# Attention weights read straight from PSUM: the copy to SBUF on ScalarE is dropped in a fused attention and FFN kernel

## The chip, the cores and the metric

One Trainium2 chip, 8 cores. Each core runs the same program on its own 4096 of the 32768 tokens; nothing is exchanged between cores. The metric is the device time of the slowest core in microseconds (us). Engines: PE is TensorE, DVE is VectorE, ACT is ScalarE, POOL is GpSimd, SP is SyncE. "Granted clock" is TensorE's clock as a share of 2.4 GHz.

## The reference

```python
q = x @ Wq + bq;  kv = (x @ Wdown + bdown) @ Wup + bup        # 16 heads of 64
att = softmax(einsum('bthd,btgd->bthg', rope(q), rope(k)) / 8)  # heads against heads, per token
out = einsum('bthg,btgd->bthd', att, v) @ Wout + bout
x = layernorm(x + out)
h = silu(x @ wg.T) * (x @ wu.T)                                 # 1024 -> 3072
x = layernorm(x + h @ wd.T)
```

Attention is between the 16 heads of one token, so there is no token by token score matrix: each token has 16 x 16 weights. The rotation of q and k by one token's own position leaves their product as it is, so the kernel leaves it out.

## The kernel before

Activations lie transposed, features on the 128 partitions and tokens along the free dimension. After a stage that casts the weights to bf16 (until about 340 us), a core works through 8 tiles of 512 tokens. `XC` is 8, the number of 128-feature blocks; `HF` is 256, half a tile.

Per tile s there are two streams of work. The main chain: `plan_head` (x load, latent and q projections), then for each half `hf` K and V (`plan_kv_part`), the scores (`plan_sc`), the weighted sum (`plan_av`) and the output projection (`plan_wo`), then the first layer norm. The second stream, `plan_ffn_ch2`, is the FFN of tile s-1: gate (L388, PSUM bank P0) and up (L398, P1) projections, `h = silu(gate) * up` (ScalarE L407, VectorE L414), down projection (L441, P2), second layer norm. The first layer norm of tile s waits for the second of tile s-1. Tile 0's attention has no FFN beside it, and the last FFN no attention.

`plan_av` works as follows. For a head the exponentials `e_sb` lie on 16 partitions (one per query head). For each block J of 128 features (two query heads) and each pair gp of key heads, one matmul with the selection matrix `selz_sb` (L707) spreads 16x512 weights over the 128 partitions into bank P5 or P6, alternating. ScalarE copies them as bf16 to `erep[gp % 2]` (L680). VectorE multiplies with the values `vdup` into `p_sb[gp % 2]` (L663). Two matmuls with the identity `id_sb` (L723) add the halves of `p_sb` into bank P7; after 8 pairs VectorE copies P7 to `avn` (L667). So a half has 8 x 8 = 64 such steps, and the kernel 1024. The order on PE within a block is b0 b1 b2 g0 g1 b3 g2 g3 b4 g4 g5 ... b7 g10 g11 g12 ... g15, where b is a broadcast and two g belong to one step.

P5 and P6 serve the projections, K, V, scores and output projection too, each of which waits for the last reader of the bank.

The order in which each engine issues is computed when the program is built. Every operation is added with `add(stream, fn, waits, inc, d=...)`, where d is its assumed cost in ns (default PE 260, VectorE 510, ScalarE 700; the summing matmuls 152, the ScalarE copy 810). The main chain and the FFN each keep their own order on each engine; a list scheduler merges the two. It takes next the operation that can start earliest by these costs, in classes of 100 ns, and among equal ones that with the longest remaining path:

```python
key = (round(es / 100.0), -CP[id(nd)], es)
if best is None or key < best[0]:
    best = (key, k, ch, nd, es)
```

At run time each engine executes its list in order, waiting on semaphores.

Of the kernel before, what the change touches and what calls it, by code (L numbers as in the profile page):

```python
# [11 lines left out]
AF = mybir.ActivationFunctionType  # L12
# [13 lines left out]
XC = D // 128  # L26
# [16 lines left out]
def build_nc(nst=NST):  # L43
# [30 lines left out]
    with ctx:  # L74
# [56 lines left out]
        s_pe = Sem(ctx, nc, "s_pe")  # L131
# [141 lines left out]
        def plan_head(s):  # L273
            t0 = s * ST
            xcast_c = []
            for c in range(XC):
                w = []
                if c == 0:
                    if ck['kv_pe_end']:
                        w.append((s_pe, ck['kv_pe_end']))  # L280
                    if ck['wo_stt_end']:
                        w.append((s_v, ck['wo_stt_end']))
                dst = x_bf[:, c * ST:(c + 1) * ST]
                src = xt[c * 128:(c + 1) * 128, t0:t0 + ST]
                w = [(s_x[c % 2], s_x[c % 2].c)] + w
                add('G', (lambda e, d=dst, sr=src: e.dma_start(d, sr)),
                    waits=w, inc=s_x[c % 2], n=16)
                xcast_c.append((s_x[c % 2], s_x[c % 2].c))
            xc_store[s] = xcast_c

            pe0 = s_pe.c
            for m in range(2):
                for c in range(XC):
                    w = []
                    if m == 0:
                        w.append(xcast_c[c])
                        if c == 0:
                            if ck['erep_end']:
                                w.append((s_s, ck['erep_end']))
                            if ck['avn_h1']:  # L300
                                w.append((s_v, ck['avn_h1']))
                    o = P[5 + m][:, :]
                    l = wd_sb[:, m * 1024 + c * 128:m * 1024 + (c + 1) * 128]
                    r = x_bf[:, c * ST:(c + 1) * ST]
                    add('T', (lambda e, o=o, l=l, r=r, st=(c == 0), sp=(c == XC - 1):
                              e.matmul(o, l, r, start=st, stop=sp)),  # L306
                        waits=w, inc=(s_pe if c == XC - 1 else None))
            lat_evac = []
            for m in range(2):
                w = [(s_pe, pe0 + m + 1)]  # L310
                if m == 0 and ck['kv_pe_end']:
                    w.append((s_pe, ck['kv_pe_end']))
                o, i_ = lat_bf[:, m * ST:(m + 1) * ST], P[5 + m][:, :]
                b = bdn_sb[:, m:m + 1]
                lat_evac.append(add('S', (lambda e, o=o, i=i_, b=b:
                                          e.activation(o, i, AF.Identity, bias=b)),
                                    waits=w, inc=s_s))
            lat_done = s_s.c

            ld0 = [s_ld[0].c, s_ld[1].c]  # L320
            pe0, sc0 = s_pe.c, s_s.c
            for m in range(XC):
                w = []
                if m < 2:
                    if ck['wqb_rd']:
                        w.append((s_pe, ck['wqb_rd']))
                else:
                    w.append((s_pe, pe0 + m - 1))
                dst, src = wqb[m % 2][:, :], wq_s[:, m * 1024:(m + 1) * 1024]
                dma('Y', s_ld[m % 2], dst, src, w)  # L330
            for m in range(XC):
                w = [(s_ld[m % 2], ld0[m % 2] + 16 * (m // 2 + 1))]
                w.append((s_s, lat_done if m < 2 else sc0 + m - 1))
                for c in range(XC):
                    o = P[5 + m % 2][:, :]
                    l = wqb[m % 2][:, c * 128:(c + 1) * 128]
                    r = x_bf[:, c * ST:(c + 1) * ST]
                    add('T', (lambda e, o=o, l=l, r=r, st=(c == 0), sp=(c == XC - 1):
                              e.matmul(o, l, r, start=st, stop=sp)),  # L339
                        waits=(w if c == 0 else ()), inc=(s_pe if c == XC - 1 else None))  # L340
            ck['wqb_rd'] = s_pe.c
            q_evac_v = []
            for m in range(XC):
                w = [(s_pe, pe0 + m + 1)]
                if m == 0 and ck['had_end']:
                    w.append((s_v, ck['had_end']))
                o, i_ = q_sb[:, m * ST:(m + 1) * ST], P[5 + m % 2][:, :]
                b = bq_sb[:, m:m + 1]
                q_evac_v.append(add('S', (lambda e, o=o, i=i_, b=b:
                                          e.activation(o, i, AF.Identity, bias=b)),  # L350
                                   waits=w, inc=s_s))
            ck['q_evac_last'] = q_evac_v[-1]
            return q_evac_v[-1]
# [161 lines left out]
        for s in range(nst):  # L515
# [30 lines left out]
            prev_wout_v = [0] * XC  # L546
            prev_avn_end_hf0 = 0

            def plan_kv_part(hf, part):
                pe0, sc0 = s_pe.c, s_s.c  # L550
                wgt = wupk_sb if part == 0 else wupv_sb
                for g in range(NH):
                    w = []
                    if g < 2:
                        w += list(wT([]))
                    if sc0 + g - 1 > 0:
                        w.append((s_s, sc0 + g - 1))
                    for c in range(2):
                        o = P[5 + g % 2][:, 0:HF]
                        l = wgt[:, g * 256 + c * 128:g * 256 + (c + 1) * 128]  # L560
                        r = lat_bf[:, c * ST + hf * HF:c * ST + hf * HF + HF]
                        add('T', (lambda e, o=o, l=l, r=r, st=(c == 0), sp=(c == 1):
                                  e.matmul(o, l, r, start=st, stop=sp)),  # L563
                            waits=(w if c == 0 else ()), inc=(s_pe if c == 1 else None), d=152)
# [62 lines left out]
            def plan_av(hf, exp_end, kv_evac_g, guard=()):  # L627
# [7 lines left out]
                v_norm = v0 + 4  # L635
                v_tt = lambda J, gp: v0 + 4 + J * 9 + gp + 1
                v_avn = lambda J: v0 + 4 + (J + 1) * 9
                s_evac = lambda lin: sc0 + lin + 1

                eap = e_sb[0:16, 0:NH * HF].rearrange("p (g t) -> p t g", g=NH)  # L640
                add('V', (lambda e, o=esum32[:, :], i=eap:
# [10 lines left out]
                prev_esum_v = s_v.c  # L652
                for J in range(XC):
                    for gp in range(8):
                        w = [(s_s, s_evac(J * 8 + gp))]
                        if gp >= 2:
                            w.append((s_pe, pe_gsum(J, 2 * gp - 3)))
                        elif J >= 1:
                            w.append((s_pe, pe_gsum(J - 1, 13 + 2 * gp)))
                        o = p_sb[gp % 2][:, :]  # L660
                        a = erep[gp % 2][:, :]
                        b = vdup[hf][:, gp * 512:(gp + 1) * 512]
                        add('V', (lambda e, o=o, a=a, b=b: e.tensor_mul(o, a, b)),  # L663
                            waits=w, inc=s_v)
                    o = avn[:, J * HF:(J + 1) * HF]
                    i_ = P[7][:, 0:HF]
                    add('V', (lambda e, o=o, i=i_: e.tensor_copy(o, i)),  # L667
                        waits=[(s_pe, pe_gsum(J, NH - 1)), (s_v, s_v.c)], inc=s_v)
                ck['avtt_end'][hf] = v_tt(XC - 1, 7)
                prev_avn_end = s_v.c  # L670
                for J in range(XC):
                    for gp in range(8):
                        lin = J * 8 + gp
                        w = list(wS([(s_pe, pe_bcast(J, gp))]))
                        if lin >= 2:
                            J2, gp2 = divmod(lin - 2, 8)
                            w.append((s_v, v_tt(J2, gp2)))
                        o = erep[gp % 2][:, :]
                        i_ = P[5 + gp % 2][:, :]
                        add('S', (lambda e, o=o, i=i_: e.activation(o, i, AF.Identity)),  # L680
                            waits=tuple(w), inc=s_s, d=810)
                erep_end = s_s.c
                for J in range(XC):
                    sched = [('b', 0), ('b', 1), ('b', 2), ('g', 0), ('g', 1)]
                    for gp in range(3, 8):
# [3 lines left out]
                    for kind, idx2 in sched:  # L689
# [8 lines left out]
                        if kind == 'b':  # L698
                            gp = idx2
                            lin = J * 8 + gp  # L700
                            if lin >= 2:
                                w.append((s_s, s_evac(lin - 2)))
                            o = P[5 + gp % 2][:, :]
                            l = selz_sb[:, J * 128:(J + 1) * 128]
                            r = e_sb[:, gp * 512:(gp + 1) * 512]
# [18 lines left out]
                                waits=w, inc=s_pe, d=152)  # L724
                assert s_pe.c == pe0 + XC * 24
                assert s_v.c == v0 + 4 + XC * 9
                assert s_s.c == sc0 + XC * 8
                prev_av_pe_end = s_pe.c
                if hf == 0:
                    prev_avn_end_hf0 = prev_avn_end  # L730
# [49 lines left out]
            vd0 = plan_kv_part(0, 1)  # L780
            exp_end0, had0 = plan_sc(0, kd0)
            avn_end0, erep_end0 = plan_av(0, exp_end0, vd0)
            kd1 = plan_kv_part(1, 0)
            vd1 = plan_kv_part(1, 1)
            exp_end1, had1 = plan_sc(1, kd1)
            wo0 = plan_wo(0, avn_end0, [(s_s, exp_end1)])
            avn_end1, erep_end1 = plan_av(1, exp_end1, vd1, [(s_v, wo0[-1])])
            wo1 = plan_wo(1, avn_end1, [(s_s, erep_end1)])
            ck['kv_pe_end'] = s_pe.c
            ck['had_end'] = had1  # L790
            ck['avn_h1'] = avn_end1
# [258 lines left out]
```

How the kernel before makes its waits and increments, by code:

```python
            @blk.sync  # L144
            def _(sync):
                srcs = [(bq_sb[:, :], bq_d[:, :]), (bdn_sb[:, :], bdn_d[:, :]),
                        (bupk_sb[:, :], bupk_d[:, :]), (bupv_sb[:, :], bupv_d[:, :]),
                        (bout_sb[:, :], bout_d[:, :]), (cvec_sb[:, :], cvec_d[:, :]),
                        (stg[0][:, 0:128], selred_d[:, :]),
                        (stg[0][:, 128:256], ones_d[:, :]),
                        (stg[0][:, 256:384], id_d[:, :]),
                        (stg[1][0:16, 0:1024], selz_d[:, :])]
                for j, (dst, src) in enumerate(srcs):
                    s_ld[j % 2].inc(sync.dma_start(dst, src), 16)
                sync.wait_ge(s_ld[0].h, s_ld[0].c)
                sync.wait_ge(s_ld[1].h, s_ld[1].c)
# [38 lines left out]
            @blk.sync  # L195
            def _(sync):
                for j, (src, soff, dt, kind, dst, doff) in enumerate(pieces):
                    if j >= 2:
                        sync.wait_ge(s_v.h, v0 + j - 1)
                    dstap = stg[j % 2][:, :]
                    if dt == I32:
                        dstap = dstap.bitcast(I32)
                    s_ld[j % 2].inc(sync.dma_start(dstap, src[:, soff:soff + 1024]), 16)
# [1 line left out]
            @blk.vector  # L205
            def _(vector):
                for j, (src, soff, dt, kind, dst, doff) in enumerate(pieces):
                    vector.wait_ge(s_ld[j % 2].h, ld0[j % 2] + 16 * (j // 2 + 1))
                    srcap = stg[j % 2][:, :]
                    if dt == I32:
```

## Time and profile before

| | us |
|---|---|
| median of the runs | 3688.32 (3687.78 to 3688.86) |
| the profiled execution | 3682.43 |
| its span on the slowest core | 3680.8 |
| spans of the 8 cores | 3661.5 to 3680.8 |
| mean granted clock of the cores | 0.898 to 0.903 |

The profile is of one execution on the slowest core. In its views a row of several equal instructions ("x2") gives the start of the first and their united busy time; rows of matmuls overlap, so the distance of starts is the better measure of PE. A line number is that of the kernel's source. An idle time is put down to what ended it.

### The profile page before, as it was taken

To read this page: it belongs to the slowest core of one execution; us is meant where nothing else is said; L and a number is where in the kernel's file an instruction comes from. 1 tells how busy PE (TensorE), PEld (TensorE's weight loads), DVE (VectorE), ACT (ScalarE), POOL (GpSimd) and SP (SyncE) were. 2 spreads that over 40 slices of the span, in tenths; PEclk is the share of its full clock that TensorE was granted. 3 is DMA by queue.
4 is the path that set the end of the run, shared out by engine and by line. 5 is a ranking of instruction groups with operands and counts; after the bars stand their busy time and mean duration, and the time that the engine had idled before them with its cause. 6 is when DMAs were issued, how large, how long until landed. Compare 5 with 4: busy or idle time off the path is not lost.

```text
span 3680.8 us, 44636 instructions; the slowest of 8 cores (3661.5 to 3680.8 us)
## 1 busy us (share of the span) xinstructions
PE 2729.1 (74%) x12447; PEld 1088.1 (30%) x12672; DVE 1465.2 (40%) x2246; ACT 1366.8 (37%) x2353; POOL 292.3 (8%) x540
## 2 busy tenths in 40 slices
PE   0001787788877988698968896898779897889666
PEld 0000222233333333233323332333333333333222
DVE  2221434354444434444335343544444444544302
ACT  0000353355334624363445442563346343534201
POOL 0111000001000110001000100011000100110010
PEclk9999756789988999999988998899989998899778
DMA  7886000212241133212231224113321332122322
GB/s 199 242 240 180 21 1 24 60 39 64 84 102 43 52 89 91 71 48 83 79 93 41 83 75 106 35 52 97 88 62 48 89 89 69 52 83 73 95 77 86
DMA packets 108728, 304.16 MB, mean 83 GB/s; under 512 B 16192, under 2 KB 24768, under 8 KB 108496
## 3 DMA queue, kind: packets, MB, share of 16 engines
q1 hardware_dynamic: 61520, 169.14, 16.3%
q0 software_dynamic: 46976, 132.15, 12.7%
q8 instruction: 118, 1.93, 0.2%
q14 instruction: 114, 0.93, 0.1%
HBM read 269.77 MB, written 39.85 MB: 84 GB/s over the span
## 4 chain that ended last, share of the span: by engine, by line
PE 56%; DMA 13%; issue 8%; ACT 7%; DVE 6%; another core or an unknown queue 0%; SPq 0%; DVEq 0%; ACTq 0%; POOL 0%; POOLq 0%
PE P L441 9%; PE P L707 8%; PE P L398 8%; PE P L388 8%; PE P L723 7%; PE P L622 7%; PE P L563 4%; DMA x_bf<-xt 3%; DMA wgb<-wg_s 3%; DMA wub<-wu_s 3%; DMA wqb<-wq_s 2%; ACT erep L680 2%; PE P L339 2%; PE P L762 2%; DVE esum L642 2%
## 5 line engine op out<-in xcount | busy, mean ns | idle before, releaser
L680 ACT ACTIVATE erep<-P 128x512 bf16<-128x512 f32 x1024 | 602.5, 597 | 635.4 <-PE P L707 458.8
L663 DVE TENSOR_TENSOR p_sb<-erep,vdup 128x512 bf16<-128x512 bf16 x1024 | 432.9, 425 | 563.8 <-PE P L723 272.1
L388 PE MATMUL P<-x_bf,wgb 128*128 128x512 bf16 x1458 | 494.0, 422 | 136.3 <-DMA wub<-wu_s 115.3
L398 PE MATMUL P<-x_bf,wub 128*128 128x512 bf16 x1466 | 512.1, 410 | 36.0 <-DVE h_sb L414 33.2
L723 PE MATMUL P<-p_sb,id_sb 128*128 128x256 bf16 x2048 | 464.9, 296 | 22.7 <-DVE p_sb L663 15.4
L707 PE MATMUL P<-e_sb,selz_sb 16*128 16x512 bf16 x1024 | 418.4, 422 | 67.2 <-DVE e_sb L650 46.4
L441 PE MATMUL P<-h_sb,wdb 128*128 128x512 bf16 x1482 | 443.0, 381 | 14.0 <-DVE r_bf L450 10.5
L597 DVE TENSOR_TENSOR hadb<-q_sb,krep 128x2048 bf16<-128x2048 bf16 x256 | 310.4, 1224 | 350.1 <-ACT krep L578 181.5
L306 PE MATMUL P<-x_bf,wd_sb 128*128 128x512 bf16 x127 | 59.0, 564 | 418.2 <-DMA x_bf<-xt 416.7
L622 PE MATMUL P<-hadb,selred_sb 128*16 128x256 bf16 x2048 | 322.9, 279 | 47.4 <-ACT e_sb L609 20.2
L414 DVE TENSOR_TENSOR h_sb<-s_sil,P 128x512 bf16<-128x512 bf16 x192 | 131.4, 684 | 460.8 <-PE P L398 253.2
L407 ACT ACTIVATE s_sil<-P 128x512 bf16<-128x512 f32 x192 | 114.4, 596 | 449.0 <-PE P L388 448.4
L762 PE MATMUL P<-avn,wob 128*128 128x256 bf16 x1024 | 237.9, 286 | 36.7 <-DMA wob<-wout_s 23.0
L388 PEld LDWEIGHTS P<-x_bf,wgb 128*128 128x128 bf16 x1536 | 147.7, 104 | 364.2 <-issue 293.5
L723 PEld LDWEIGHTS P<-p_sb,id_sb 128*128 128x128 bf16 x2048 | 179.1, 100 | 244.5 <-issue 164.7
L398 PEld LDWEIGHTS P<-x_bf,wub 128*128 128x128 bf16 x1536 | 151.3, 102 | 257.7 <-issue 183.8
L256 POOL DMA_DIRECT2D wgb<-wg_s x192 | 105.1, 547 | 1498.2 <-PE P L398 1385.8
L622 PEld LDWEIGHTS P<-hadb,selred_sb 128*16 128x16 bf16 x2048 | 157.2, 90 | 201.8 <-issue 174.5
L707 PEld LDWEIGHTS P<-e_sb,selz_sb 16*128 16x128 bf16 x1024 | 88.3, 92 | 366.7 <-issue 366.6
L339 PE MATMUL P<-x_bf,wqb 128*128 128x512 bf16 x504 | 134.2, 416 | 81.9 <-DMA wqb<-wq_s 68.3
L609 ACT ACTIVATE e_sb<-P,cvec_sb 16x256 bf16<-16x256 f32 x256 | 116.4, 464 | 197.4 <-PE P L622 196.8
L441 PEld LDWEIGHTS P<-h_sb,wdb 128*128 128x128 bf16 x1536 | 127.8, 97 | 177.6 <-issue 87.6
(65 smaller groups left out, 1913.2 us busy)
## 6 DMA issues: line engine op xcount, KB each, us to landing
wdb<-wdn_s SPq DMA_DIRECT2D x64, 768.0 KB, 4.3
wgb<-wg_s POOLq DMA_DIRECT2D x192, 256.0 KB, 3.0
wub<-wu_s POOLq DMA_DIRECT2D x192, 256.0 KB, 3.0
wob<-wout_s SPq DMA_DIRECT2D x128, 256.0 KB, 2.9
wqb<-wq_s SPq DMA_DIRECT2D x64, 256.0 KB, 3.1
yt<-x2b SPq DMA_DIRECT2D x64, 256.0 KB, 3.4
stg<-wg SPq DMA_DIRECT2D x24, 512.0 KB, 5.3
stg<-wu SPq DMA_DIRECT2D x24, 512.0 KB, 5.2
```

The lines of the kernel that those rows point to most:

```text
L339: e.matmul(o, l, r, start=st, stop=sp)),
L388: e.matmul(o, l, r, start=st, stop=sp)),
L398: e.matmul(o, l, r, start=st, stop=sp)),
L441: e.matmul(o, l, r, start=st, stop=sp)),
L563: e.matmul(o, l, r, start=st, stop=sp)),
L597: add('V', (lambda e, o=o, a=q3, b=b: e.tensor_mul(o, a, b)), waits=tuple(w), inc=s_v, d=1460)
L622: e.matmul(o, l, r, start=st, stop=sp)),
L663: add('V', (lambda e, o=o, a=a, b=b: e.tensor_mul(o, a, b)), waits=w, inc=s_v)
L680: add('S', (lambda e, o=o, i=i_: e.activation(o, i, AF.Identity)), waits=tuple(w), inc=s_s, d=810)
L707: e.matmul(o, l, r, start=True, stop=True)),
L723: e.matmul(o, id_sb[:, :], r, start=st, stop=sp)),
L762: e.matmul(o, l, r, start=st, stop=sp)),
```

## The change

The copies on ScalarE (L680) are dropped. The product on VectorE takes P5 or P6 as its first operand, in fp32. Its waits become the broadcast matmul itself and, in the first block, the evacuated values; its assumed cost becomes 640. Broadcast lin waits for product lin-2 in place of copy lin-2. What used to wait for the last copy (`erep_end`) waits for the last `avn` copy: the K matmuls of the second half by a new `guard`, the second output projection, and the next tile's head, which had that wait already. The tensors `erep` remain allocated.

```diff
@@ plan_head @@
-                            if ck['erep_end']:
-                                w.append((s_s, ck['erep_end']))
@@ plan_kv_part @@
-            def plan_kv_part(hf, part):
+            def plan_kv_part(hf, part, guard=()):
...
                     if g < 2:
                         w += list(wT([]))
+                        w += list(guard)
@@ plan_av @@
-                        w = [(s_s, s_evac(J * 8 + gp))]
+                        w = [(s_pe, pe_bcast(J, gp))]
+                        if J == 0:
+                            w.append((s_s, kv_evac_g[2 * gp + 1]))
...
-                        a = erep[gp % 2][:, :]
+                        a = P[5 + gp % 2][:, :]
                         b = vdup[hf][:, gp * 512:(gp + 1) * 512]
                         add('V', (lambda e, o=o, a=a, b=b: e.tensor_mul(o, a, b)),
-                            waits=w, inc=s_v)
+                            waits=w, inc=s_v, d=640)
...
-                for J in range(XC):
-                    for gp in range(8):
-                        lin = J * 8 + gp
-                        w = list(wS([(s_pe, pe_bcast(J, gp))]))
-                        if lin >= 2:
-                            J2, gp2 = divmod(lin - 2, 8)
-                            w.append((s_v, v_tt(J2, gp2)))
-                        o = erep[gp % 2][:, :]
-                        i_ = P[5 + gp % 2][:, :]
-                        add('S', (lambda e, o=o, i=i_: e.activation(o, i, AF.Identity)),
-                            waits=tuple(w), inc=s_s, d=810)
-                erep_end = s_s.c
+                erep_end = prev_avn_end
...
                             if lin >= 2:
-                                w.append((s_s, s_evac(lin - 2)))
+                                J2, gp2 = divmod(lin - 2, 8)
+                                w.append((s_v, v_tt(J2, gp2)))
@@ tile loop @@
-            kd1 = plan_kv_part(1, 0)
+            kd1 = plan_kv_part(1, 0, guard=[(s_v, avn_end0)])
...
-            wo1 = plan_wo(1, avn_end1, [(s_s, erep_end1)])
+            wo1 = plan_wo(1, avn_end1, [(s_v, erep_end1)])
```

## Rows read from the trace of the kernel before

**Rows 1.** The page: span, and busy time of two engines
```profile
span 3680.8 us, 44636 instructions; the slowest of 8 cores (3661.5 to 3680.8 us)
...
PE 2729.1 (74%) x12447; PEld 1088.1 (30%) x12672; DVE 1465.2 (40%) x2246; ACT 1366.8 (37%) x2353; POOL 292.3 (8%) x540
```

**Rows 2.** Busy by stage: start:end, length, PE, PEld, DVE, ACT, POOL, clock, DMA, GB/s
```profile
2352.00:2422.00 70.00, 67.32 (x285) 23.43 (x292) 33.81 (x78) 40.20 (x70) 6.57 (x12) 0.90 0.15 43
...
2480.00:2522.00 42.00, 31.68 (x162) 15.73 (x164) 20.23 (x21) 6.67 (x11) 7.13 (x13) 0.96 0.43 121
2522.00:2606.00 84.00, 81.08 (x364) 31.04 (x373) 33.36 (x76) 38.30 (x66) 3.82 (x7) 0.98 0.24 75
```

**Rows 3.** Timeline, PE in av1: start us, length us, engine, line, operation
```profile
2392.07 0.38 PE L707 MATMUL P<-e_sb,selz_sb 16*128 16x512 bf16 x1
2392.39 0.39 PE L398 MATMUL P<-x_bf,wub 128*128 128x512 bf16 x1
...
2392.61 0.38 PE L723 MATMUL P<-p_sb,id_sb 128*128 128x256 bf16 x2
2392.93 0.38 PE L707 MATMUL P<-e_sb,selz_sb 16*128 16x512 bf16 x1
```

**Rows 4.** Timeline, first and last of seven avn copies (av1, av2), of eight (tile 0)
```profile
2366.18 0.42 DVE L667 CAST avn<-P 128x256 bf16<-128x256 f32 x1 [2.03 <-PE P L723]
...
2414.00 0.42 DVE L667 CAST avn<-P 128x256 bf16<-128x256 f32 x1 [0.70 <-PE P L723]
...
2535.54 0.42 DVE L667 CAST avn<-P 128x256 bf16<-128x256 f32 x1 [0.72 <-PE P L723]
...
2598.26 0.42 DVE L667 CAST avn<-P 128x256 bf16<-128x256 f32 x1 [0.71 <-PE P L723]
...
449.86 0.42 DVE L667 CAST avn<-P 128x256 bf16<-128x256 f32 x1 [0.91 <-PE P L723]
...
516.47 0.42 DVE L667 CAST avn<-P 128x256 bf16<-128x256 f32 x1 [0.90 <-PE P L723]
```

**Rows 5.** Groups by line, 2370 to 2420 us, then 2540 to 2600 us
```profile
L663 DVE TENSOR_TENSOR p_sb<-erep,vdup 128x512 bf16<-128x512 bf16 x51 | 21.3, 424 | 17.5 <-PE P L707 8.8 <-ACT erep L680 7.9 <-PE P L723 0.5
...
L398 PE MATMUL P<-x_bf,wub 128*128 128x512 bf16 x35 | 12.0, 384 | 0.2 <-issue 0.2
L388 PE MATMUL P<-x_bf,wgb 128*128 128x512 bf16 x34 | 11.1, 384 | 0.2 <-issue 0.2
...
L441 PE MATMUL P<-h_sb,wdb 128*128 128x512 bf16 x125 | 38.7, 382 | 0.5 <-issue 0.3 <-DVE p_sb L663 0.2
```

**Rows 6.** Groups by line, whole span: count, busy us, mean ns, idle before and what ended it
```profile
L680 ACT ACTIVATE erep<-P 128x512 bf16<-128x512 f32 x1024 | 602.5, 597 | 635.4 <-PE P L707 458.8 <-DVE p_sb L663 92.3 <-DVE avn L667 77.3
...
L663 DVE TENSOR_TENSOR p_sb<-erep,vdup 128x512 bf16<-128x512 bf16 x1024 | 432.9, 425 | 563.8 <-PE P L723 272.1 <-ACT erep L680 207.9 <-PE P L707 78.1
...
L414 DVE TENSOR_TENSOR h_sb<-s_sil,P 128x512 bf16<-128x512 bf16 x192 | 131.4, 684 | 460.8 <-PE P L398 253.2 <-ACT s_sil L407 205.3 <-remote 2.3
```

**Rows 7.** Timeline, tile 0 at half clock: PE's cadence, then the end of a block
```profile
463.88 0.60 PE L707 MATMUL P<-e_sb,selz_sb 16*128 16x512 bf16 x1
...
464.42 0.61 PE L723 MATMUL P<-p_sb,id_sb 128*128 128x256 bf16 x2
...
464.96 0.60 PE L707 MATMUL P<-e_sb,selz_sb 16*128 16x512 bf16 x1
...
467.55 0.43 DVE L663 TENSOR_TENSOR p_sb<-erep,vdup 128x512 bf16<-128x512 bf16 x1 [0.65 <-PE P L723]
468.13 0.59 PE L723 MATMUL P<-p_sb,id_sb 128*128 128x256 bf16 x2 [0.49 <-DVE p_sb L663]
...
468.89 0.42 DVE L667 CAST avn<-P 128x256 bf16<-128x256 f32 x1 [0.91 <-PE P L723]
```

**Rows 8.** Busy by stage, tile 0's first weighted sum; columns as in Rows 2
```profile
441.00:515.00 74.00, 66.74 (x189) 13.84 (x188) 29.77 (x70) 37.16 (x64) 0.00 (x0) 0.50 0.00 1
```

More of the change, by code:

```diff
@@ L637, in plan_av @@
                 v_avn = lambda J: v0 + 4 + (J + 1) * 9
-                s_evac = lambda lin: sc0 + lin + 1
                 eap = e_sb[0:16, 0:NH * HF].rearrange("p (g t) -> p t g", g=NH)
@@ L726, in plan_av @@
                 assert s_v.c == v0 + 4 + XC * 9
-                assert s_s.c == sc0 + XC * 8
                 prev_av_pe_end = s_pe.c
```

## Prediction

> **What bounds the kernel now.** I read the page first: 3680.8 us, of which TensorE (PE) is busy 2729 and VectorE 1465 [rows 1]. A share over the whole span doesn't say what one stage is bound by, so I read the busy time of one tile's stages next [rows 2]. Each tile walks the attention chain twice (halves hf 0 and 1), and each half has a weighted-sum stage made by `plan_av`. I call them av1 (2352 to 2422 us in this tile) and av2 (2522 to 2606). PE shows 67.3 of 70 us in av1 and 81.1 of 84 in av2: there it is nearly full, while VectorE has 33.8 and 33.4. Between them, at 2480 to 2522, PE has 31.7 of 42 and the transfers their largest share: the feed-forward (FFN) weights arrive too slowly there.
>
> How full PE is has to be counted in starts, because rows of matmuls overlap. Call a step one broadcast matmul (L707), one product on VectorE (L663) and its two summing matmuls (L723). In av1 the broadcast starts, 0.32 us later an FFN matmul, 0.22 us later the summing pair, and 0.32 us later the next broadcast [rows 3]. So the chain takes 0.32 + 0.32, with finer starts 0.63 us of PE a step, and each FFN matmul 0.22.
>
> A block J is 8 steps and ends in one `avn` copy, so the distance of these copies is the time of a block. In av1 it is (2414.00 - 2366.18)/6 = 7.97 us, in av2 (2598.26 - 2535.54)/6 = 10.45 us [rows 4]. FFN matmuls between: in av1 34 + 35 beside 51 products, that is 10.8, say 11 a block; in av2 125 in 60 us, 21.8 a block [rows 5]. PE's own need is then 8 x 0.63 + 11 x 0.22 = 7.46 us in av1 and 5.04 + 4.80 = 9.84 in av2. Both stages are PE's with some 0.5 us of holes at each block's end. ScalarE's hop costs 597 ns a step but hides: two steps are in flight.
>
> **The change, part by part.**
> *ScalarE's copies go.* 1024 x 597 ns, 602.5 us of ScalarE [rows 6]. On the path they are worth only the holes, at most (7.97 - 7.46) x 56 = 29 us in av1 and (10.45 - 9.84) x 56 = 34 us in av2 (56 blocks each, tiles 1 to 7), since PE is full otherwise.
>
> *VectorE's product reads fp32 from PSUM.* 128x512 bf16 from SBUF alone takes 425 ns. The nearest row with one operand in PSUM is the FFN product L414, same size and output, 684 ns [rows 6]. I take 684: +259 ns x 1024 = 265 us of VectorE. Bounds: 425 (no price) and 684 with nothing gained, as no row of this shape is longer. As busy time it fits: av1 would have 33.8 + 64 x 0.26 = 50.4 of 70 us.
> The Trainium skill ("Perfetto Trace Analysis", section "Optimizing Scalar/DVE Operations") advises moving work to ScalarE where VectorE is saturated. By busy share alone VectorE isn't saturated here and the move would cost nothing; the sum below finds a cost from the order of waits. The share of this trace agrees with the page's premise and can't decide the rest.
>
> *The waits.* Today a PSUM bank comes free when ScalarE has copied it. Afterwards broadcast lin+2 waits for product lin, and product lin+2 waits for broadcast lin+2 and for summing pair lin (the `p_sb` buffer). Handoffs: the product of 467.55 ends at 467.98 and the pair starts at 468.13, 0.15 us; that pair ends at 468.72 and VectorE starts at 468.89, 0.17 us [rows 7]. A loop over two steps at full clock: product 0.684 + 0.15 + broadcast 0.32 + pair from start to end 0.38 [rows 3] + 0.17 = 1.70 us, 0.85 a step. A block: 0.6 from first to second product (VectorE back to back, estimate from 684 ns less overlap) + 3 x 1.70 + the block's end. The end is: last product 0.684 + 0.15 + pair 0.38 + 0.17 + `avn` copy 0.43 + 0.05 = 1.86. Together 7.56, and the FFN products, some 0.4 a block at 0.69, make it 7.8 us. So VectorE's loop replaces PE as the bound of av1, at nearly the old block time (7.97).
>
> *The planner.* The emitted order of each engine follows from the costs in the code. Before: a block is 8 x 810 on ScalarE + 510 + 304 + 260 = 7554 ns; PE's chain work in it is 8 x 260 + 16 x 152 = 4512; the rest holds 3042/260 = 11.7 FFN matmuls, and the trace has 11. So the planner lets the chain go first in av1 and fills its gaps. With 640 on VectorE, working the same costs: inside a block one FFN matmul per two steps fits (3), and at the block's end, where PE waits for pair, `avn` and the next product, about 4 more. That makes 7, and 4512 + 7 x 260 = 6.3 us a block. The 4 that are displaced from each block cost 4 x 0.22 = 0.88 us later, where PE is full (av2) or the weights are late. In av2 FFN matmuls go first or alternate; PE stays the bound (9.8 against a loop of 7.8), so I cost it at nothing. What hides the loop there is those 22 matmuls; without them it would be av1's case.
> Sum per block of av1: 7.8 - 7.97 + 0.88 = +0.71; x 56 = +40 us. Ends: 7.5 us and only 1.5 displaced gives -8 us; 8.3 and 5 displaced gives +80.
>
> *Tile 0* has no FFN to fill with, and runs at a granted clock of 0.50 [rows 8], 1.2 GHz. Broadcast to pair is 0.54 us and pair to broadcast 0.54 [rows 7]. A block is (516.47 - 449.86)/7 = 9.52 us [rows 4]. Afterwards: loop 0.684 + 0.15 + 0.54 + 0.59 + 0.17 = 2.13; block 0.6 + 6.4 + 0.684 + 0.15 + 0.59 + 0.17 + 0.48 = 9.1. That is -0.4 x 16 = -7 us.
>
> *The new guard.* The second half's K matmuls wait for the last `avn` (L667) instead of the last copy: 0.17 + 0.43 + 0.15 = 0.75 us at most, queued behind it all of PE's chain; 8 x 0.75 = +6 us, zero if FFN matmuls fill it. I take +5. The guards `erep_end` of `plan_wo` and `plan_head` become the `avn` wait they already had: nothing. No DMA is moved.
>
> Sum: +40 - 7 + 5 = +38 on the profiled execution's 3682.4 (span 3680.8), 3720; this execution lies 6 us under the median of 3688.3, so 3726.
>
> **The rivals.**
> *A, likeliest: av1 passes from PE to VectorE's loop and FFN work is displaced.* 3690 to 3762. 50%.
> *B, the order stays as rich as now.* If the planner keeps about 11 FFN matmuls a block, the result is 7.8 - 7.97 = -0.17 x 56 = -10 us, with tile 0 -7: 3670; within 3615 to 3690. For it: the same matmuls must be placed somewhere, and the FFN's remaining path may come first earlier. 18%.
> *C, the holes close in both stages.* -29 - 34 - 7 = -70, 3618 us; only with a little from the other stages over 2%. Against it: the loop of 7.56 is over PE's need, and the 1.86 at each block's end stays. 7%.
> *D, VectorE's queue.* FFN products stand in order behind attention products that wait for PE, and PE's next up-projection waits for the FFN product (one bank each). 640 planned against 684 and handoffs of 0.15 and 0.17 that the plan doesn't have: no slack, where ScalarE had 810 planned against 597. If each block pays one such stall of 0.7 to 1.0 us, +40 to +56 over A: 3765 to 3785. 12%.
> *E, the clock (the slow side).* Tile 0's stage has PE rows busy 66.7 of 74 us and still gets 0.50 [rows 8]; av1, with 11 FFN matmuls a block between, gets 1.00 after its start. With 7, av1 lies between the two. At 1.2 GHz a block is 8 x 1.08 + 7 x 0.43 = 11.7 us; if half of av1's blocks run so, (11.7 - 7.8) x 28 = +109 over A, 3835; all of them, 3940. It decides as soon as a sixth of the blocks is cold (3.9 x 9 = +36 over A, past 3762). Against it: matmul columns per us fall only from (8 x 1024 + 11 x 512)/7.97 = 1730 to 11776/7.8 = 1510. 13%.
> The Trainium skill ("TensorE: Matmul & The Clock Gate", section "What's actually happening") calls the throttled clock the default, which activity releases. By that rule alone av1, which has no long hole, stays at 2.4 GHz and E is nil. This trace agrees for the stages with FFN work, but tile 0 shows that activity with few idle gaps isn't enough.
>
> **How the numbers follow.** The predicted time is A's, 3726 us. From 3650 (inside B) to 3830 (the half of E): A 50, most of B 15, D 12, a little of E 4, in all 8 in 10. About 2% is what a measurement of this kernel can tell from no change: under 3615 or over 3762. Faster is C, if it comes with a little more from other stages: 0.07. Slower is D and E: 0.25. Within 2%: 0.68.
>
> **What would show it.** Product L663 at 684 ns (right) or much less (my price is wrong). `avn` distance in av1 7.5 to 8.3 us, with about 7 FFN matmuls a block. VectorE's idle before the product ended by L707 and L723, PE's idle before L707 ended by `p_sb` L663. av2 still at 10.4 or a little longer, with more FFN matmuls. Granted clock in av1 1.00; 0.5 to 0.8 would be E. PE's wait for `h_sb` L414, now small, grown to tens of us would be D. What makes the prediction wrong: blocks of av1 at 7.5 or less with 11 FFN matmuls still in them, or stages besides av1 that move, since the planner orders all anew.

## The result and the profile after

The changed kernel takes 3737.9 us (median) against 3691.2 us of the kernel before, measured beside it: a ratio of 1.0138, 95% interval 1.0103 to 1.0174. It is slower by 1.4%, less than 2%. The medians are of all executions; the ratio leaves out those in which some cores fell into a slower state of the chip.

The page of its slowest core, and the rows that answer to [rows 1] and [rows 6]; line numbers have moved: the broadcast is L697 (was L707), the summing matmuls L713 (L723), the FFN's projections L386 and L396, its product L412.

```profile
span 3732.3 us, 40735 instructions; the slowest of 8 cores (3669.1 to 3732.3 us)
...
PE 2788.5 (75%) x12447; PEld 1094.4 (29%) x12672; DVE 1723.8 (46%) x2246; ACT 774.0 (21%) x1331; POOL 293.1 (8%) x540
...
L663 DVE TENSOR_TENSOR p_sb<-P,vdup 128x512 bf16<-128x512 f32 x1024 | 694.3, 690 | 370.1 <-PE P L713 337.1
...
L396 PE MATMUL P<-x_bf,wub 128*128 128x512 bf16 x1465 | 505.4, 411 | 6.0 <-DVE h_sb L412 3.9
```

The product went from 425 to 690 ns, VectorE gained 259 us, ScalarE lost 593. Three of the eight cores (span, mean granted clock):

```profile
core 1: 3730.9 us, clock 0.879
core 2: 3732.3 us, clock 0.880
...
core 5: 3669.1 us, clock 0.895
```

The cores, which do the same work, now lie 63 us apart; before it was 19, at clocks of 0.898 to 0.903. The slowest has the lowest clock but one. So the next view is busy time and clock between neighbouring `avn` copies of one tile, that is block by block, on core 2 (start:end, length, PE, PEld, DVE, ACT, POOL, clock, DMA, GB/s). The first five rows are blocks of av1, the last is seven blocks of av2:

```profile
2002.91:2015.36 12.45, 11.93 (x33) 3.10 (x33) 6.46 (x10) 0.60 (x1) 1.10 (x2) 0.50 0.14 42
2015.36:2026.72 11.36, 11.36 (x32) 2.92 (x31) 5.87 (x9) 0.00 (x0) 0.00 (x0) 0.50 0.00 0
2026.72:2039.35 12.63, 12.27 (x34) 3.37 (x34) 6.46 (x10) 0.60 (x1) 1.10 (x2) 0.50 0.14 43
2039.35:2052.46 13.11, 12.98 (x37) 3.54 (x36) 6.46 (x10) 0.00 (x0) 1.10 (x2) 0.53 0.08 21
2052.46:2061.70 9.24, 9.01 (x43) 3.23 (x42) 6.41 (x10) 0.60 (x1) 0.76 (x2) 1.00 0.20 55
...
2198.10:2264.23 66.13, 63.73 (x289) 23.29 (x293) 43.52 (x70) 1.26 (x2) 0.00 (x0) 1.00 0.22 69
```

Four blocks run at 1.2 GHz (clock 0.50 or near it) and take 11.4 to 13.1 us; the fifth has 2.4 GHz and takes 9.24 us though it holds more matmuls (43 rows against 32 to 37). In the kernel before such a block took 7.97 us, the mean of six [rows 4]. Seven blocks of av2 take 66.1 us, against 62.7 for six before, so 9.4 a block instead of 10.45. Below, a block or stage at 1.2 GHz is called cold and one at 2.4 GHz warm, and a distance of two `avn` copies in av1 of over 10.8 us is counted as a cold distance. Tiles 1 to 7 have 49 such distances a core, 392 on eight cores. Core 5 (span 3669) has 11 cold ones, core 2 (3732) has 18, all cores together 117; before, no core had any.

Where the time went, as sums over tiles 1 to 7 between `avn` copies, in us, mean of the eight cores. "Mid" goes from the last copy of av1 to the first of av2; "head" from the last of av2 to the first of the next av1, so the first block of a stage lies in the column ahead of it. The last two rows belong to experiments told below.

```
kernel                 av1    mid    av2    head    sum
before               392.4  809.6  514.7  1009.7  2726.5
changed              494.0  805.5  466.2   993.9  2759.7
changed, warm (e1)   431.4  809.4  464.8   971.4  2677.0
before, warm (e5)    394.2  818.1  515.0   986.1  2713.3
```

The change costs 101.6 us in av1 and gives back 68.4 elsewhere, +33 over these tiles; over the whole span the mean core goes from 3671.3 to 3701.9, +31. The metric takes the slowest core: the profiled execution (3733.9 us) lies 32 us over that mean, before (3682.4) 11 us, another 21. That makes the +51 us.

The order that the planner emitted explains the stages. FFN matmuls in each of the eight blocks of av1 and of av2, in a middle tile (tiles 3 and 4 of the changed kernel; its others differ somewhat), and in the K and V stages between the halves:

```
kernel                      av1                          K, V      av2
before                      13 11 12 13 13 10 12 13      15   8    29 29 23 22 23 22 24 24
changed                      7  9  7 10 12 17 18 18      25  30    20 17 16 19 20 17 16 19
changed, cost 810 (e2)      11 12  9 13 12 13 10 13      16   7    29 27 22 21 22 21 24 23
before, cost 640 (e3)        6  9  7  9  8 17 19 16      28  30    34 17 19 20 19 18 17 20
```

### The profile page after: what moved, and what is told of

The parts are those of the page before. It is cut to its first block, busy times and chain, and to the rows that moved or that the text cites. A ratio compares the mean times of both kernels' runs of the same rounds, so it can differ in the third digit from the quotient of the medians.

```text
span 3732.3 us, 40735 instructions; the slowest of 8 cores (3669.1 to 3732.3 us)
## 1 busy us (share of the span) xinstructions
PE 2788.5 (75%) x12447; PEld 1094.4 (29%) x12672; DVE 1723.8 (46%) x2246; ACT 774.0 (21%) x1331; POOL 293.1 (8%) x540
## 3 DMA queue, kind: packets, MB, share of 16 engines
q0 software_dynamic: 46976, 132.15, 12.6%
## 4 chain that ended last, share of the span: by engine, by line
PE 59%; DMA 14%; DVE 8%; issue 6%; ACT 3%; another core or an unknown queue 0%; SPq 0%; POOL 0%; DVEq 0%; ACTq 0%; POOLq 0%
PE P L697 10%; PE P L439 9%; PE P L713 9%; PE P L396 8%; PE P L386 7%; PE P L621 7%; DMA wgb<-wg_s 4%; DMA x_bf<-xt 3%; DMA wub<-wu_s 3%; PE P L562 3%; DMA wqb<-wq_s 2%; PE P L337 2%; PE P L751 2%; DVE p_sb L663 2%; DVE esum L640 2%
## 5 line engine op out<-in xcount | busy, mean ns | idle before, releaser
L663 DVE TENSOR_TENSOR p_sb<-P,vdup 128x512 bf16<-128x512 f32 x1024 | 694.3, 690 | 370.1 <-PE P L713 337.1
L386 PE MATMUL P<-x_bf,wgb 128*128 128x512 bf16 x1465 | 502.3, 425 | 132.7 <-DMA wub<-wu_s 113.7
L697 PE MATMUL P<-e_sb,selz_sb 16*128 16x512 bf16 x1024 | 451.0, 451 | 97.7 <-DVE e_sb L648 72.5
L713 PE MATMUL P<-p_sb,id_sb 128*128 128x256 bf16 x2048 | 496.3, 314 | 25.1 <-DVE p_sb L663 17.7
L396 PE MATMUL P<-x_bf,wub 128*128 128x512 bf16 x1465 | 505.4, 411 | 6.0 <-DVE h_sb L412 3.9
L439 PE MATMUL P<-h_sb,wdb 128*128 128x512 bf16 x1476 | 459.8, 381 | 14.2 <-DVE r_bf L448 13.5
L412 DVE TENSOR_TENSOR h_sb<-s_sil,P 128x512 bf16<-128x512 bf16 x192 | 131.5, 685 | 406.9 <-PE P L396 262.0
L751 PE MATMUL P<-avn,wob 128*128 128x256 bf16 x1024 | 230.4, 284 | 34.8 <-DMA wob<-wout_s 20.2
L386 PEld LDWEIGHTS P<-x_bf,wgb 128*128 128x128 bf16 x1536 | 154.9, 105 | 326.8 <-issue 246.7
L713 PEld LDWEIGHTS P<-p_sb,id_sb 128*128 128x128 bf16 x2048 | 163.7, 102 | 271.3 <-issue 238.8
L697 PEld LDWEIGHTS P<-e_sb,selz_sb 16*128 16x128 bf16 x1024 | 91.0, 93 | 465.1 <-issue 465.1
L396 PEld LDWEIGHTS P<-x_bf,wub 128*128 128x128 bf16 x1536 | 152.4, 103 | 209.9 <-issue 120.1
L439 PEld LDWEIGHTS P<-h_sb,wdb 128*128 128x128 bf16 x1536 | 141.4, 97 | 194.7 <-issue 98.4
L762 DVE SCALAR_TENSOR_TENSOR r_bf<-P,bout_sb,x_bf 128x256 bf16<-128x256 f32 x128 | 61.7, 482 | 254.6 <-PE P L751 254.6
L217 DVE CAST stgb<-stg 128x1024 bf16<-128x1024 int32 (+1 forms) x88 | 61.1, 694 | 224.8 <-DMA wu_s<-stgb 50.9
```

The source lines that it names most:

```text
L412: h_v.append(add('V', (lambda e, o=o, a=a, b=b: e.tensor_mul(o, a, b)), waits=w, inc=s_v2, d=780))
L663: add('V', (lambda e, o=o, a=a, b=b: e.tensor_mul(o, a, b)), waits=w, inc=s_v, d=640)
L697: e.matmul(o, l, r, start=True, stop=True)),
L713: e.matmul(o, id_sb[:, :], r, start=st, stop=sp)),
```

## The experiments

Each ratio is to the kernel before, measured beside it. Theories at the start: the clock (E of the prediction, which the profile now spoke for) and displacement (A).

**e1: warm start.** Ten matmuls whose result nobody reads, while VectorE still normalizes the exponentials, just ahead of the first broadcast; P7 is overwritten by the first summing matmul.

```diff
+                for _i in range(10):
+                    add('T', (lambda e, o=P[7][:, :], r=x_bf[:, 0:ST]:
+                              e.matmul(o, id_sb[:, :], r, start=True, stop=True)),
+                        waits=[(s_v, v0 + 1)] if _i == 0 else [])
                 for J in range(XC):
                     sched = [('b', 0), ('b', 1), ('b', 2), ('g', 0), ('g', 1)]
```

> The changed kernel with ten extra matmuls (identity times a slice of x, into bank P7, which is overwritten afterwards) between the reduction of the exponentials and the first broadcast of every weighted sum; they compute nothing that is used, and the order of all else stays. Clock theory: the changed kernel is slower because the first two to four blocks of av1 run at 1.2 GHz (12.5 us instead of 7.5 to 8.3). With PE busy just before, they start at 2.4 GHz: first blocks 7.5 to 8.3 us, no block of 12, spans of the cores alike, time 3640 to 3670 us, under the kernel before. Displacement theory (VectorE's loop and the FFN matmuls that were moved cost the time, the cold blocks are incidental): 3700 to 3740 us.

Measured: ratio 0.9906 (0.9886 to 0.9926), against 1.0138 without the ten matmuls. Busy time and clock on core 3: from the end of the reduction to past the ten matmuls, then three blocks of av1.

```profile
1911.00:1919.00 8.00, 7.76 (x30) 2.66 (x28) 7.17 (x8) 0.60 (x1) 0.55 (x1) 0.88 0.11 33
1923.33:1931.12 7.79, 7.30 (x35) 2.38 (x33) 6.18 (x10) 0.60 (x1) 1.09 (x2) 1.00 0.22 67
1931.12:1938.62 7.50, 6.92 (x33) 2.19 (x31) 5.72 (x9) 0.00 (x0) 0.00 (x0) 1.00 0.00 0
1938.62:1946.41 7.79, 7.51 (x36) 2.48 (x34) 6.18 (x10) 0.60 (x1) 1.09 (x2) 1.00 0.23 68
```

The same blocks, with the same number of matmul rows give or take two, take 7.5 to 7.8 us instead of 11.4 to 12.6. On eight cores 17 distances are cold instead of 117; av1 is 63 us shorter and "head", in which the first block lies, 22 us. So displacement alone doesn't explain the loss.

The expectation was met in the time, but not in full: it had no block of 12 us and equal spans, and the spans still lie 43 us apart (3593.3 to 3636.7). Three cores have no cold distance, the others 2 to 6, in two kinds of place. In tile 1 av1 began cold on cores 1, 4 and 7 and turned cold in its first block on core 2. On four cores the clock fell in the third block of one later tile (7 FFN matmuls) and stayed down for the next two.

Nor did the order of all else stay, as the expectation has it. Between the last scores and the first broadcast the changed kernel has 10 FFN matmuls in tiles 1, 2, 5 and 7 and 25 in the others; e1 has 10 in tile 1 and 25 in all others, besides the ten. Tiles 1, 3 and 4 have the same order in both up to av1's last two blocks. There the cold distances fall from 70 of 168 to 13.

**e8: the control.** The same ten matmuls, but without the wait, so that they issue before the reduction and PE is mostly idle behind them.

```diff
-                        waits=[(s_v, v0 + 1)] if _i == 0 else [])
+                        waits=[])
```

> e1 with the ten extra matmuls issued before the reduction of the exponentials instead of behind it, so that PE stands idle between them and the first broadcast. The control for e1: same count, same bank, same order of all else. Clock theory: the clock has fallen again by the first broadcast, the first blocks of av1 are cold as in the changed kernel (11 to 13 us), ratio 1.005 to 1.018. If the extra matmuls helped in some other way: ratio 0.99 as in e1.

Measured: ratio 1.0148 (1.0111 to 1.0186), the changed kernel's. On core 7, the pause (PE busy 4.14 of 12 us), the chain's first 4 us, and two blocks of av1:

```profile
1969.00:1981.00 12.00, 4.14 (x19) 1.67 (x17) 11.02 (x4) 2.34 (x3) 1.09 (x2) 0.84 0.14 44
1981.00:1985.00 4.00, 3.40 (x8) 0.64 (x8) 2.23 (x4) 0.00 (x0) 0.00 (x0) 0.50 0.00 0
1993.17:2005.81 12.64, 12.64 (x35) 3.38 (x34) 6.46 (x11) 0.60 (x1) 1.09 (x2) 0.50 0.14 43
2005.81:2018.63 12.82, 12.82 (x37) 3.52 (x35) 6.46 (x11) 0.00 (x0) 0.55 (x1) 0.52 0.06 20
```

So it isn't the ten matmuls as such, but PE at work right ahead of the first broadcast. The control isn't clean in every tile: the planner moved FFN matmuls too, and e8 has only 9 or 10 of them ahead of the first broadcast in tiles 2 to 7, where e1 has 25. In tile 1 the two orders differ in nothing but the place of the ten. There av1 began warm on five of eight cores in e1 and on none in e8, with 9 and 18 cold distances (17 in the changed kernel).

**e5: is it the change, or only the warm start?** The ten matmuls of e1 in the kernel before.

> The kernel before with the same ten extra matmuls ahead of each weighted sum (they compute nothing that is used): what a warm start alone is worth without the change. The kernel before spends about 14 us of each av1 at 1.2 GHz, some 5 us lost in each of 7 tiles and less in av2. If the change has a gain of its own that the clock hid (holes closed in av1 and av2): this kernel at 0.992 to 0.998 of the kernel before, and the changed kernel with the same ten matmuls (e1, 0.9906) under it. If all of e1's gain is the warm start: 0.990 or less, the same as e1.

Measured: ratio 0.9974 (0.9953 to 0.9994). A warm start is worth 0.3% there. By the table that is 24 us less in "head" and 8 more in "mid", where the ten matmuls ahead of av2 lie; whether they are those 8 us wasn't separated. With both kernels warm, the change is worth 0.9906/0.9974 = 0.993, a gain of 0.7% or some 25 us; the two intervals together leave about 0.990 to 0.996. The clock turned that into a loss: 1.0138/0.9906 = 1.023.

**e2: the old order with the new product.**

```diff
-                            waits=w, inc=s_v, d=640)
+                            waits=w, inc=s_v, d=810)
```

> The changed kernel with the product's assumed cost 810 in place of 640, so that the planner gives each block of av1 9 to 13 FFN matmuls as in the kernel before. Clock theory: PE is full at 1.2 GHz too and the clock rises as before; blocks of av1 8.0 to 8.3 us from the second on, time 3650 to 3690 us. Displacement theory: with 11 FFN matmuls between, VectorE's loop makes a block 8.5 us or more, time 3700 to 3730 us.

Measured: ratio 1.0063 (1.0041 to 1.0085), between the two theories. Core 5, the same block in two tiles, then the two blocks that follow the second:

```profile
1176.48:1184.45 7.97, 7.83 (x38) 2.67 (x36) 5.77 (x9) 0.60 (x1) 0.55 (x1) 1.00 0.12 35
1567.06:1580.55 13.49, 13.49 (x37) 3.68 (x36) 5.87 (x9) 0.60 (x1) 0.56 (x1) 0.50 0.07 21
1580.55:1593.00 12.45, 12.36 (x34) 3.10 (x33) 6.46 (x10) 0.60 (x1) 1.09 (x2) 0.50 0.14 42
1593.00:1606.68 13.68, 13.68 (x39) 3.82 (x37) 6.45 (x10) 0.00 (x0) 1.09 (x2) 0.52 0.12 33
```

Warm, a block is mostly 7.65 to 7.97 us with 9 to 13 FFN matmuls, faster than the kernel before's: VectorE's loop, which displacement put at 8.5 or more, doesn't bind. But the clock theory missed too: it said that a full PE would bring the clock back at once. Here PE is busy for all of 13.49 us and stays at 1.2 GHz, for three such distances in a row. That happened in none to three of the seven tiles, by core: 36 cold distances in all.

**e6: both**, the cost of 810 and the ten matmuls.

> The changed kernel with the product's cost at 810 and the ten extra matmuls: warm, with 9 to 13 FFN matmuls in each block of av1. If its losses in e2 (blocks of 13.5 us in some tiles of each core) were the clock: blocks 7.7 to 8.0 throughout av1, ratio 0.985 to 0.993 to the kernel before. If the thin order of the changed kernel is what costs even when warm (displaced FFN matmuls): this one is faster than e1 by 10 us or more. If displaced matmuls find holes elsewhere: equal to e1 within 0.3%.

Measured: ratio 0.9907 (0.9884 to 0.9929), the same as e1. On six cores all distances are 7.64 to 7.97 us (8.26 once each). Cores 2 and 7 have three cold ones each, of 12.5 to 13.7 us, in tile 6. It is the only tile of e6 with 10 FFN matmuls ahead of the first broadcast besides the ten; the others have 25. A warm block, on core 3:

```profile
1950.07:1957.96 7.89, 7.80 (x38) 2.67 (x36) 5.77 (x9) 0.60 (x1) 0.55 (x1) 1.00 0.18 59
```

The thin order of e1 and the rich one of e6 end at the same time, within the intervals of 0.2% or some 8 us each; 49 us were charged for the displacement. So the displaced FFN matmuls cost nothing that shows: they went into av1's last blocks and the K and V stages (25 and 30 in place of 15 and 8), and av2 became shorter by what it lost.

**e3: the thin order without the new product.**

```diff
-                            waits=tuple(w), inc=s_s, d=810)
+                            waits=tuple(w), inc=s_s, d=640)
```

> The kernel before, copy on ScalarE kept, with that copy's assumed cost 640 in place of 810: the order gets 5 to 9 FFN matmuls in each of the first five blocks of av1, like the changed kernel. Clock theory: the first blocks fall to 1.2 GHz here too, 11 to 13 us each on some cores, time 3720 to 3770 us. Displacement theory: without VectorE's long product nothing is lost, 3675 to 3700 us.

Measured: ratio 1.0082 (1.0060 to 1.0104). The first row is a warm block of av1, the second a cold one of another tile, on one core:

```profile
1991.18:1999.03 7.85, 7.37 (x35) 2.42 (x33) 4.26 (x10) 4.67 (x8) 1.09 (x2) 1.00 0.23 68
788.76:800.97 12.21, 12.21 (x34) 3.22 (x33) 4.42 (x11) 4.67 (x8) 1.09 (x2) 0.50 0.15 43
```

The kernel before, with ScalarE's copies in place, falls to 1.2 GHz in the same way once its order is thinned: 67 cold distances on eight cores. One assumed cost in the planner is enough. The size is below the expected 3720 to 3770 us (3707.8): core 3, the core of these rows, had none to three cold distances a tile. Nor is all of the loss av1's. In the table's columns it has 444.8, 848.1, 465.7 and 992.0 us: av1 takes 52 us more than before and "mid" 38 more, whose end is av2's first block, now with 34 FFN matmuls instead of 29; av2 and "head" give back 67.

**e4: the long product alone.** The copies stay and the order is unchanged; `erep` is fp32, so the product reads four bytes an element from SBUF.

```diff
-        erep = [E(nc.sbuf_tensor(f"erep{i}", [128, 512], BF16)) for i in range(2)]
+        erep = [E(nc.sbuf_tensor(f"erep{i}", [128, 512], F32)) for i in range(2)]
```

> The kernel before with erep in fp32, so that the product takes about 690 ns instead of 425, order and hop unchanged. If VectorE's longer product by itself costs time: a block grows by 0.26 us at its end (av1 8.3, av2 10.7, tile 0 9.8), +30 us. If PE hides it: within 0.3% of the kernel before. In neither case a change of the clock.

Measured: ratio 1.0187 (1.0168 to 1.0205). The groups, and the first and last of eight `avn` copies in tile 0, then in one av1:

```profile
L663 DVE TENSOR_TENSOR p_sb<-erep,vdup 128x512 bf16<-128x512 f32 x1024 | 697.3, 691 | 385.4 <-PE P L723 197.5 <-ACT erep L680 141.3 <-PE P L707 39.2
L680 ACT ACTIVATE erep<-P 128x512 f32<-128x512 f32 x1024 | 602.4, 597 | 700.3 <-PE P L707 518.5 <-DVE avn L667 100.2 <-DVE p_sb L663 75.5
...
450.43 0.42 DVE L667 CAST avn<-P 128x256 bf16<-128x256 f32 x1 [0.91 <-PE P L723]
520.81 0.42 DVE L667 CAST avn<-P 128x256 bf16<-128x256 f32 x1 [0.91 <-PE P L723]
...
2414.11 0.42 DVE L667 CAST avn<-P 128x256 bf16<-128x256 f32 x1 [1.00 <-PE P L723]
2474.93 0.42 DVE L667 CAST avn<-P 128x256 bf16<-128x256 f32 x1 [0.70 <-PE P L723]
```

A block is 70.38/7 = 10.05 us in tile 0 (9.52 before) and 60.82/7 = 8.69 in av1 (7.97). So 266 ns more on VectorE aren't hidden behind PE when ScalarE's 597 ns are in the chain too: +0.5 and +0.7 us a block. With the hop gone they are: 9.50 and, in e6, 7.86. The effect was foreseen, its size was not: 0.26 us a block and +30 us were expected, and 1.87% is some 69 us. Nor did the clock stay out of it, as expected: four cores have 11 cold distances between them, late in av1, where the kernel before has none.

**e7: can tile 0 be warm?** e1 with 12 matmuls a block into the idle bank P0, in tile 0 alone.

```diff
+                            for _i in range(1 + gp % 2 if s == 0 else 0):
+                                add('T', (lambda e, o=P[0][:, :], r=x_bf[:, 0:ST]:
+                                          e.matmul(o, id_sb[:, :], r, start=True, stop=True)))
```

> e1 with, in tile 0 alone, 12 further matmuls in each block of the weighted sums (identity times a slice of x into the idle bank P0, unused), in the place that the FFN's have in the later tiles. Clock theory: tile 0 runs at 1.2 GHz because nothing fills PE between the chain's matmuls; filled, it goes at 2.4 GHz, its blocks 7.6 to 8.2 us instead of 9.5, 20 to 30 us less than e1. If tile 0 is cold for another reason: blocks of 13 to 14 us and 60 us more than e1.

Measured: ratio 0.9970 (0.9942 to 0.9999), 0.6% worse than e1. Core 4, the first half's weighted sum of tile 0 and the second's, the same instructions in both:

```profile
451.00:513.00 62.00, 54.92 (x247) 19.63 (x251) 40.48 (x63) 0.00 (x0) 0.00 (x0) 1.00 0.00 1
602.00:702.00 100.00, 94.67 (x246) 24.97 (x251) 41.67 (x63) 0.00 (x0) 0.00 (x0) 0.50 0.00 0
```

Both of the expected cases occurred, on one core. The first half held 2.4 GHz (8.89 us a block, over the expected 7.6 to 8.2), the second 1.2 GHz for 100 us (14.38 us a block). Of the 16 weighted sums of tile 0 on eight cores ten were warm, four cold to the end, and two left 1.2 GHz after three blocks. The mean block of tile 0 is 10.5 us, against 9.52 in e1, so the fill lost on the mean core too, and the metric takes the unluckiest.

## Why the prediction was right and its reason wrong

The predicted 3726 us (+1.0%) stands beside a measured +1.4%, inside the range and the likeliest class. That is luck, for the sum was right by two errors that cancelled: case A, which carried it, isn't what happened; a gain of 25 us came true, and E, which had 13%, on top of it.

- *The product's price*, 684 ns: right, 690. (That no row of this shape is longer wasn't so: the kernel before has VectorE rows of 128x512 with 692 ns.)
- *The block of av1*, 7.5 to 8.3 us with about 7 FFN matmuls: right where the clock is 2.4 GHz. Blocks with 9, 7 and 10 take 7.79, 7.50 and 7.79 us in e1. The planner's sum gave 7 and the order has 7 to 10 in the first blocks. It failed from the fifth block on (12 to 18), where the FFN's remaining path comes first. I had taken one block for all eight.
- *Displaced matmuls at 0.88 us a block* is the step that failed; 0.88 x 56 = 49 us, it was more than all of the +40. I charged them where PE is full. e1 and e6 show that they cost nothing measurable. They left av2 as well, which I had said would stay at 10.4 us or grow: it fell to 9.4. The K and V stages took in 32 more of them, and "mid", in which they lie, didn't grow (809.6 and 805.5 us); av2's first block, which lies there too, has 9 fewer.
- *The holes* (C, at most 63 us in av1 and av2): the change is worth 25 us once both kernels are warm. But e6 (389.5, 808.3, 508.9 and 979.2 us in the table's columns) is under e5 by 5 us in av1, 10 in "mid", 6 in av2 and 7 in "head". So less than half of it lies where C had put it, and no run shows that it is holes.
- *Tile 0*, -7 us: nothing, 9.52 and 9.50 us a block. By e4 the longer product costs 0.53 us there with the hop kept; leaving out the hop gave back just that.
- *The guard*, +5 us: 2.5. The K matmuls' wait for `avn` on core 2 (us, times):

```profile
  DVE avn L667: 2.5, 8
```

- *D, VectorE's queue*: nil. PE waited 3.9 us for the FFN product in all, as the page's L396 row shows, and 33.2 us before:

```profile
L398 PE MATMUL P<-x_bf,wub 128*128 128x512 bf16 x1466 | 512.1, 410 | 36.0 <-DVE h_sb L414 33.2 <-issue 2.3
```

- *E, the clock*: price and place right, 11.7 us a block predicted and 11.4 to 12.6 measured with 7 to 10 matmuls. With 117 of 392 distances cold, E's own price gives 0.30 x 56 x 3.9 = 65 us, and e1 took 63 off av1. The chance was too low. I argued from matmul columns per us at full clock whether a warm stage would *stay* warm; the question was mostly in which state it *starts* (e1's four later falls and e4's eleven cold distances show that staying isn't sure either). The profile had the sign: av1 follows VectorE's reduction, for part of which PE idles, and its first block ran partly at 1.2 GHz in the kernel before too. The tile's av1 shows 0.90 over 70 us [rows 2]; parted at its first `avn` copy:

```profile
2352.00:2366.00 14.00, 13.62 (x37) 4.10 (x39) 4.39 (x10) 4.67 (x8) 0.55 (x1) 0.50 0.07 20
2366.00:2422.00 56.00, 53.69 (x250) 19.32 (x255) 29.42 (x68) 35.53 (x62) 6.02 (x11) 1.00 0.17 49
```

  By the Trainium skill ("TensorE: Matmul & The Clock Gate", section "What's actually happening") the slow clock is the default and activity releases it. I read that as speaking against E. The traces of e1 (1.00 with PE busy ahead) and e8 (0.50 behind the pause) agree with it at the start of av1. e2 and e7 show its limit: PE was busy 13.49 of 13.49 us and 94.7 of 100 us without being released.

What stays open: what in the order lets the kernel before leave 1.2 GHz within its first block, while e2, with nearly the same order (11 matmuls in the first block instead of 13) and no ScalarE hop, sometimes needs four. No run separates the count, the way the matmuls are grouped, and the missing hop. Nor is it known what the ten matmuls need beside them: with 25 FFN matmuls ahead of the first broadcast av1 began warm in all 96 stages of e1 and e6, with 10 in 7 of 16. Nor is the spread between cores all av1: from core 5 to core 2, 31 of the 63 us lie in av1's distances and 10 in a later start of tile 0's; the rest is spread over the other stages.

## What to carry to other kernels

Where two chains share PE, an assumed cost in the planner decides how full PE is in each stage, and with it the clock: compare the kernels' granted clock stage by stage before crediting or blaming an engine. Here av1, which begins behind a pause of PE, mostly started at half clock and could stay there, so a gain of 0.7% became a loss of 1.4%. A few matmuls nobody needs at the end of the pause turned it into a gain of 0.9%, and the changed kernel with them (e1, e6) is the fastest one measured here. A longer operation isn't hidden because the other engine is full; it is hidden if the loop through it is shorter than that engine's. e4 and e6 fit that from both sides, though the loop of e4 wasn't worked out.

## What the runs showed of the hardware

- The instruction stream alone doesn't set the granted clock. In e7 the same stream on the same core ran 62 us at 1.00 (8.89 us a block) and 100 us at 0.50 (14.38), and PE's busy share was higher in the slow one. Of 16 such stages 14 kept from their start to their end the clock they began with.
- Full occupation of PE at 1.2 GHz doesn't bring back 2.4 GHz by itself: 13.49 us busy of 13.49, 12.36 of 12.45 and 13.68 of 13.68, three blocks in a row at 0.50 to 0.52 (e2).
- Ten matmuls in the last microseconds of a pause, with the FFN matmuls that the planner put ahead of them, start the next stage at 2.4 GHz: in 53 of 56 stages of av1 in e1, against 7 of 56 in the changed kernel without them. With the ten ahead of the pause it was none of 56 (e8).
- A VectorE product of 128x512 takes 690 ns with its fp32 operand in PSUM and 691 ns with it in SBUF (e4); 425 ns all in bf16.
